# Seam columns of u*B made ahead on ScalarE and POOL and copied in by ScalarE, with 27 products a chunk on POOL, in a one-core Mamba block

## The chip, the cores and the metric

The kernel runs on one core of one Trainium2 chip. The metric is the device time of one execution in microseconds (us); lower is better. The core has a tensor engine (TensorE, PE in the profile), a vector engine (VectorE, DVE), a scalar engine (ScalarE, ACT), GpSimd (POOL) and SyncE (SP), whose queue issues most DMAs. Each engine runs its own list of instructions in order, and they wait for each other on semaphores.

## The reference

Two batches of 2048 rows of width 512 go through a block with adaptive layer norms. The first half is a Mamba mixer, the second a sum of 8 matrices. What matters here is the mixer:

```python
h = layernorm(x) * (1 + ca) + sa
h, gate = split(h @ in_proj_w.T)          # 1024 channels each
h = silu(conv1d_causal(h, 4 taps) + conv_b)
dt, B, C = split(h @ x_proj_w.T)          # 128, 16, 16
dt = softplus(dt @ dt_proj_w.T + dt_proj_b)
for t in rows:                            # per channel e and state n
    s[e, n] = s[e, n] * exp(dt[t, e] * A[e, n]) + (dt[t, e] * h[t, e]) * B[t, n]
    y[t, e] = sum_n s[e, n] * C[t, n]
y = (y + h * D) * silu(gate);  x = x + ga * (y @ out_proj_w.T)
x = x + gb * (sum_r layernorm'(x) @ factors[r] / sqrt(8) + bias)
```

All of it is in 32-bit floats. `u` is dt * h, and `ub` is u * B.

## The kernel before, in words

The 4096 rows are cut into 16 chunks of 256 rows, 8 for each batch. Channels lie on the 128 partitions in 8 tiles, taken as 4 pairs (q = 0 to 3). In a chunk the state recurrence is 64 units, one for each pair q and state n. A unit is one scan over 512 elements: the 256 rows of the pair's first tile and, behind them, the 256 rows of its second. Four units are a quad (g = 0 to 15), two units are a step (s = 0 to 31, so step s lies in quad s // 2).

Each unit takes four operations:

- `decays` (ScalarE, L722): two exponentials fill one of three PSUM banks `decay` with exp(dt * A).
- `make_ub` (POOL, L568): u * B for a whole quad at once, 128x2048, into one of three slots `ub`. It is made two quads ahead.
- `scan` (VectorE, L1426): the recurrence.
- the product with C: on VectorE (`multiply_c`, L1441, into `sc_d`) for the first units of a quad, on POOL (L596, in place in `state_p`) for the last k units of a quad. k is read from the lists `EVEN_POOL`, `ODD_POOL`, `FIRST_POOL` (chunk 0), `FOLD_POOL` (chunk 1) and `LAST_POOL` (chunk 15). TensorE then turns the product back and adds it up in `y_bank` (L1010).

`keep_carry` (ScalarE, L706) keeps the last column of each state for the next chunk. `copy_y` (ScalarE, L811) takes each pair's sums out of `y_bank` at steps 2, 10, 18 and 26 of the pair after it, and TensorE can't begin on the next pair (L1001) before that.

A scan takes only one initial value, so the second tile's carry has to come in otherwise: its first decay is zeroed (L718, or skipped by the exponential), and carry * decay is added to the first column of the second tile in `ub`. That column is the seam. The kernel before does it on POOL: `seam_decays` (ScalarE, L845) writes the decays of the 16 states and a pair into `seam`, `make_seam` (POOL, L554) multiplies them by the carries for two pairs at once, in quads 0 and 4, and behind every `make_ub` POOL adds 128x4 elements of `seam` into `ub` (L582). Chunks 0 and 8 begin a batch and need no seam.

Around the units lies the other work, put between them by hand at given steps: in chunk c the projection and convolution of chunk c + 1 (`project_h` L1085, `copy_h` L766 to L775, `taps` L1481, `add_tap` L1068, `tanh_before` L787, `silu_before` L1490), its dt, B and C (`copy_dt`, `copy_bc`, `soft_dt` L835, with a reload of the activation table), and of chunk c - 1 the gate (`project_gate` L1057, `tanh_gate` L859, `silu_gate` L1500, `turn_sums` L1141, `gate_sums` L1522), the output projection (L1157, `residual_mixer` L1529) and the second half. `copy_h` of the first pair is at step 5, as is `tanh_gate` of the last pair of chunk c - 1; in ScalarE's order of before `copy_h` stands first. B and C of a chunk come back from memory spread over all partitions (`load_b` L340, in two halves), once POOL has used the old ones.

Of the kernel before, what the change touches and what calls it, by code (L numbers as in the profile page):

```python
# [57 lines left out]
EVEN_POOL = (2, 2, 2, 2, 2, 2, 2, 2, 2, 2, 2, 1, 1, 1, 1, 1)  # L58
ODD_POOL = (2, 2, 2, 2, 1, 2, 2, 2, 2, 2, 2, 1, 1, 1, 1, 1)
# [17 lines left out]
NORMS = 2 + LB  # L77

# [38 lines left out]
def seam_count(c):  # L117

    return c - c // PER

# [44 lines left out]
def build(nc, x, win_m, xp_t, dt_t, wo_t, chan, cond_t, wmod, factors, bias, out):  # L165
# [11 lines left out]
    with ExitStack() as ctx:  # L177
# [52 lines left out]
        seam = [sb(f"seam{i}", [P, N, PAIRS]) for i in range(2)]  # L230
        y_rows = sb("y_rows", [P, LB, E])
# [29 lines left out]
        ub_product, seam_decay, seam_made, seam_zeroed = sem("ub_product"), sem("seam_decay"), sem("seam_made"), sem("seam_zeroed")  # L261
# [60 lines left out]
        def _(sp):  # L322
# [10 lines left out]
            def load_b(c, par, h):  # L333

                if c:
                    sp.wait_ge(ub_made, QUADS * c - 2 * (1 - h) - 1)
                sp.wait_ge(bc_stored, 16 * c + 16)
                n0 = h * N // 2
                src = bc_dram[par, 0:1, n0 * ROWS:(n0 + N // 2) * ROWS].to_broadcast([P, N * ROWS // 2])
                sp.dma_start(b_all[:, n0:n0 + N // 2, :].rearrange("p n r -> p (n r)"), src).then_inc(b_loaded[h], 16)  # L340
# [172 lines left out]
        def _(pool):  # L513
# [33 lines left out]
            def make_seam(c, half):  # L547

                qs = slice(2 * half, 2 * half + 2)
                pool.wait_ge(seam_decay, 2 * seam_count(c) - 1 + half)  # L550
                pool.wait_ge(carried, carries_after(UNITS * (c - 1) + N * qs.stop - 1))
                odd = carry[c // PER][:, :, :].rearrange("p n (q j) -> p n q j", j=2)[:, :, qs, 1]
                part = seam[c % 2][:, :, qs]
                pool.tensor_tensor(part, part, odd, ALU.mult).then_inc(seam_made, 1)  # L554

            def make_ub(quad):
# [7 lines left out]
                if q == 0 and n % (N // 2) == 0 or quad == 1:  # L564
# [6 lines left out]
                                   ALU.mult).then_inc(ub_product if c % PER else ub_made, 1)  # L571
                if c % PER == 0:
                    return
                if g == 0:
                    make_seam(c, 0)
                    pool.wait_ge(seam_made, 2 * seam_count(c) - 1)
                if g == 4:
                    make_seam(c, 1)
                    pool.wait_ge(seam_made, 2 * seam_count(c))
                pool.wait_ge(ub_product, QUADS * (seam_count(c) - 1) + g + 1)  # L580
                first = ub[:, slot, :, 1, 0]
                pool.tensor_tensor(first, first, seam[c % 2][:, n:n + QUAD, q], ALU.add).then_inc(ub_made, 1)  # L582
# [67 lines left out]
            def one_round(c, par, la, lc):  # L650
                for g in range(QUADS):
# [7 lines left out]
                    if quad + UB_RING - 1 < QUADS * CHUNKS:  # L659
                        make_ub(quad + UB_RING - 1)  # L660
                    multiply_c(quad)
# [14 lines left out]
                    if la is not None and g == 13:  # L676
                        make_u(c + 1, 0)

# [11 lines left out]
        def _(act):  # L690
# [146 lines left out]

            def seam_decays(c, par, half):
# [3 lines left out]
                wait(act, ub_made, QUADS * (c - 1) - 1)  # L842
# [74 lines left out]
            def one_round(c, par, la, lc):  # L917
                for s in range(STEPS):
                    a = s - H_LATE if c == 0 else s
                    step = STEPS * c + s  # L920
                    pair = 2 * step // N
                    decays(2 * step)
# [18 lines left out]
                    if c == 0 and s in (7, 12):  # L941
                        rows_absolute(s // 12, (0.5, RANK ** -0.5)[s // 12])
                    if s in (4, 6, 12):
                        skip(c, {4: 1, 6: 2, 12: 3}[s])
                    if la is not None:
# [12 lines left out]
                        if s in (27, 31) and (c + 1) % PER:  # L958
                            seam_decays(c + 1, 1 - par, s // 31)
                    if c + 2 < CHUNKS and s == 30:  # L960
                        z_before(c + 2)
                    if lc is not None:
                        if s in (1, 3, 5):
                            tanh_gate(c - 1, {1: 1, 3: 2, 5: 3}[s])
# [443 lines left out]
        def _(dve):  # L1408
            def scan(unit):
# [5 lines left out]
                if unit < QUAD:  # L1415
                    dve.wait_ge(ub_first, unit + 1)
                elif i == 0:
# [312 lines left out]
```

## Time and profile before

| | |
|---|---|
| median of 3 runs | 2021.61 us (2020.21 to 2022.54) |
| the profiled execution, its time | 2025.55 us |
| the profiled execution, its span | 2023.8 us |
| mean granted TensorE clock | 0.973 |
| VectorE busy | 1867.4 us, 92% |
| POOL busy | 1835.7 us, 91% |
| TensorE matmuls busy | 1759.7 us, 87% |
| ScalarE busy | 1517.1 us, 75% |

The span is what the trace covers; the execution's own time is 1.75 us more. Busy time counts the time in which an instruction ran; two short instructions in a row overlap in the records by up to a tenth of a microsecond, so that the distance of their starts is what one costs the engine. Idle time before an instruction is given with what ended it.

### The profile page before, as it was taken

To read this page: it belongs to the slowest core of one execution; us is meant where nothing else is said; L and a number is where in the kernel's file an instruction comes from. 1 tells how busy PE (TensorE), PEld (TensorE's weight loads), DVE (VectorE), ACT (ScalarE), POOL (GpSimd) and SP (SyncE) were. 2 spreads that over 40 slices of the span, in tenths; PEclk is the share of its full clock that TensorE was granted. 3 is DMA by queue.
4 is the path that set the end of the run, shared out by engine and by line. 5 is a ranking of instruction groups with operands and counts; after the bars stand their busy time and mean duration, and the time that the engine had idled before them with its cause. 6 is when DMAs were issued, how large, how long until landed. Compare 5 with 4: busy or idle time off the path is not lost.

```text
span 2023.8 us, 29343 instructions
## 1 busy us (share of the span) xinstructions
PE 1759.7 (87%) x9128; PEld 1312.2 (65%) x9128; DVE 1867.4 (92%) x2240; ACT 1517.1 (75%) x4646; POOL 1835.7 (91%) x925
## 2 busy tenths in 40 slices
PE   7985889889889898988989888898988899898798
PEld 5664757667576765757666675766757576676564
DVE  2799989999999999999999999999999999999995
ACT  3767778697877869777786977878787786878662
POOL 1789999999999999999998999999999999999992
PEclk9897999999999999999999999999999999999798
DMA  4656514132140412304042240403223040311200
GB/s 171 235 114 153 140 48 147 31 121 79 43 143 15 152 47 97 103 30 154 17 141 68 111 141 22 157 22 131 68 73 121 28 156 22 121 53 55 92 27 32
DMA packets 72001, 186.17 MB, mean 92 GB/s; under 512 B 6818, under 2 KB 8482, under 8 KB 63908
## 3 DMA queue, kind: packets, MB, share of 16 engines
q1 hardware_dynamic: 68148, 176.95, 26.3%
q0 software_dynamic: 3696, 7.34, 2.2%
q8 instruction: 73, 1.20, 0.2%
q14 instruction: 84, 0.69, 0.1%
HBM read 172.20 MB, written 12.06 MB: 91 GB/s over the span
## 4 chain that ended last, share of the span: by engine, by line
PE 42%; ACT 19%; POOL 15%; DVE 13%; issue 9%; DMA 1%; DVEq 0%; POOLq 0%; SPq 0%; ACTq 0%
PE y_bank L1010 10%; PE bank_a L1085 10%; PE bank_c L1157 9%; POOL ub L568 8%; ACT decay L722 7%; DVE decay L1426 5%; POOL state_p L596 5%; PE bank_c L1057 4%; DVE state_p L1426 3%; PE bank_a L1068 2%; ACT dt L835 2%; DVE sc_d L1441 2%; ACT L722 2%; ACT hT L737 2%; ACT L835 2%
## 5 line engine op out<-in xcount | busy, mean ns | idle before, releaser
L568 POOL TENSOR_TENSOR ub<-u,b_all 128x2048 f32<-128x2048 f32 x255 | 1160.4, 4551 | 48.5 <-DMA b_all<-bc_scratch 47.4
L722 ACT ACTIVATE decay<-dt,decay_rate 128x256 f32<-128x256 f32 (+1 forms) x2048 | 889.6, 466 | 36.0 <-DVE state_p L1426 34.3
L1426 DVE TENSOR_TENSOR_SCAN decay<-decay,carry,ub 128x512 f32<-128x512 f32 x610 | 763.7, 1277 | 25.8 <-ACT decay L722 23.8
L596 POOL TENSOR_TENSOR state_p<-state_p,c_all 128x1024 f32<-128x1024 f32 (+1 forms) x256 | 498.7, 1948 | 85.3 <-ACT carry L706 82.4
L1426 DVE TENSOR_TENSOR_SCAN state_p<-decay,carry,ub 128x512 f32<-128x512 f32 x414 | 527.4, 1274 | 9.3 <-ACT decay L722 7.2
L1010 PE MATMUL y_bank<-ident,sc_d 128*128 128x128 f32 x2440 | 362.5, 283 | 79.9 <-DVE sc_d L1441 79.5
L1441 DVE TENSOR_TENSOR sc_d<-decay,c_all 128x512 f32<-128x512 f32 x610 | 406.7, 671 | 0.0
L1010 PEld LDWEIGHTS y_bank<-ident,sc_d 128*128 128x128 f32 x2440 | 292.9, 145 | 146.1 <-DVE sc_d L1441 120.8
L706 ACT ACTIVATE carry<-decay 128x2 f32<-128x2 f32 x610 | 100.8, 165 | 264.8 <-DVE sc_d L1441 262.9
L1010 PEld LDWEIGHTS y_bank<-ident,state_p 128*128 128x128 f32 x1656 | 195.7, 143 | 126.9 <-POOL state_p L596 71.7
L1010 PE MATMUL y_bank<-ident,state_p 128*128 128x128 f32 x1656 | 231.0, 279 | 53.2 <-POOL state_p L596 52.0
L1085 PE MATMUL bank_a<-hT,win_h 128*128 128x256 f32 x992 | 240.5, 387 | 32.4 <-DVE hc L1490 30.0
L1057 PE MATMUL bank_c<-hT,win_z 128*128 128x256 f32 x960 | 230.7, 387 | 0.0
L1157 PE MATMUL bank_c<-wo,yg 128*128 128x512 f32 x480 | 223.8, 594 | 0.0
L1085 PEld LDWEIGHTS bank_a<-hT,win_h 128*128 128x128 f32 x992 | 182.3, 193 | 58.7 <-DVE hc L1490 35.7
L1057 PEld LDWEIGHTS bank_c<-hT,win_z 128*128 128x128 f32 x960 | 181.7, 196 | 22.6
L1068 PE MATMUL bank_a<-pre_z,tap_diag 128*128 128x256 f32 x496 | 120.4, 386 | 12.2 <-DVE bank_a L1481 12.2
L1157 PEld LDWEIGHTS bank_c<-wo,yg 128*128 128x128 f32 x480 | 86.6, 191 | 67.0 <-issue 64.8
L1068 PEld LDWEIGHTS bank_a<-pre_z,tap_diag 128*128 128x128 f32 x496 | 92.7, 191 | 39.8 <-DVE bank_a L1481 15.8
L1187 PE MATMUL bank_c<-ffn,hT 128*128 128x512 f32 x240 | 115.9, 605 | 0.0
L1001 PE MATMUL y_bank<-ident,skipped 128*128 128x128 f32 x256 | 42.9, 294 | 71.5 <-ACT y_rows L811 71.5
L718 ACT ACTIVATE decay<-ident 128x1 f32<-128x1 f32 x608 | 103.4, 170 | 0.1
(139 smaller groups left out, 1842.1 us busy)
## 6 DMA issues: line engine op xcount, KB each, us to landing
win_h<-win_m SPq DMA_DIRECT2D x128, 256.0 KB, 2.6
win_z<-win_m SPq DMA_DIRECT2D x128, 256.0 KB, 2.8
b_all<-bc_scratch SPq DMA_DIRECT2D x31, 1024.0 KB, 4.7
c_all<-bc_scratch SPq DMA_DIRECT2D x31, 1024.0 KB, 6.6
xa<-x SPq DMA_DIRECT2D x16, 512.0 KB, 5.0
xc<-x SPq DMA_DIRECT2D x16, 512.0 KB, 3.8
out<-xc SPq DMA_DIRECT2D x15, 512.0 KB, 4.0
ffn<-factors POOLq DMA_DIRECT2D x7, 1024.0 KB, 10.0
```

The source lines that it names most:

```text
L568: pool.tensor_tensor(ub[:, slot, :, :, :], u[:, (PAIRS * c + q) % U_PAIRS, :, :].unsqueeze(1).to_broadcast([P, QUAD, 2, ROWS]), b_all[:, n ...
L596: pool.tensor_tensor(part, part, c_all[:, n + QUAD - k:n + QUAD, :].unsqueeze(2).to_broadcast([P, k, 2, ROWS]), ALU.mult).then_inc(pooled, 1)
L718: act.activation(bk[:, ROWS:ROWS + 1], ident[:, 0:1], ACT.Copy, scale=0.0)
L722: last = act.activation(bk[:, j * ROWS + j:(j + 1) * ROWS], dt[:, pair % DT_PAIRS, j, j:], ACT.Exp, scale=decay_rate[:, e, n:n + 1])
L1010: last = pe.matmul(y_bank[:, at:at + P], tile[:, j, t * P:(t + 1) * P], ident[:, :], start=False, stop=last_of_pair, is_transpose=True, sk ...
L1057: last = pe.matmul(dst[:, j * ROWS:(j + 1) * ROWS], tile[:, k, :], hTc[:, k, :], start=(k == 0), stop=(k == KD - 1))
L1068: last = pe.matmul(h_lane(c, q)[:, j * ROWS:(j + 1) * ROWS], tap_diag[:, i, 2 * q + j, :], pre[q % 2][:, j, k:k + ROWS], start=False, stop ...
L1085: last = pe.matmul(h_lane(c, q)[:, j * ROWS:(j + 1) * ROWS], win_h[i % H_TILES][:, k, :], hT[c % H_RING][:, k, :], start=(k == 0 and j == ...
L1157: last = pe.matmul(bank_c[t][:, :], yg[:, k, t * P:(t + 1) * P], wo[:, k, :], start=(k == 0), stop=(k == KE - 1))
L1187: last = pe.matmul(bank_c[t][:, :], hT[c % H_RING][:, k, t * P:(t + 1) * P], ffn[:, k, :], start=False, stop=(k == KD - 1))
L1426: dve.tensor_tensor_scan(dst, bk[:, :], ub[:, quad % UB_RING, i, :, :].rearrange("p j r -> p (j r)"), carried_in[:, n, 2 * q:2 * q + 1], A ...
L1441: dve.tensor_tensor(sc_d[:, i % D_RING, :, :], bk[:, :].rearrange("p (j r) -> p j r", j=2), c_all[:, n:n + 1, :].to_broadcast([P, 2, ROWS] ...
```

## The change: the seam is added to a column apart, and ScalarE copies it in

POOL no longer adds into `ub`. ScalarE makes the first column of u * B of the second tile apart (`make_column`, into a new buffer `column`, 128x16 for a pair, the first pair in two halves of 128x8). POOL multiplies carries and decays as before (`carry_seam`, now at rounds 13 and 4) and adds the columns to `seam` in four additions a chunk (`add_column`). ScalarE copies 128x4 of `seam` into the slot of `ub` ahead of the first decays of each quad (`add_seam`), and the scan waits for that copy.

With it `make_u` of the next chunk's first pair goes from round 13 to 12 on POOL, `load_b` waits for the columns too, `tanh_gate` at steps 1, 3 and 5 stands ahead of `skip`, `modulate_before`, `tanh_before` and `copy_h` of the same step, and the lists of POOL's products change: quad 7 goes from 2 to 1 and quad 13 from 1 to 2 in both lists, and in the odd chunks quad 4 goes from 1 to 2.

```diff
-EVEN_POOL = (2, 2, 2, 2, 2, 2, 2, 2, 2, 2, 2, 1, 1, 1, 1, 1)
-ODD_POOL = (2, 2, 2, 2, 1, 2, 2, 2, 2, 2, 2, 1, 1, 1, 1, 1)
+EVEN_POOL = (2, 2, 2, 2, 2, 2, 2, 1, 2, 2, 2, 1, 1, 2, 1, 1)
+ODD_POOL = (2, 2, 2, 2, 2, 2, 2, 1, 2, 2, 2, 1, 1, 2, 1, 1)
...
 def load_b(c, par, h):
                 if c:
                     sp.wait_ge(ub_made, QUADS * c - 2 * (1 - h) - 1)
+                    wait(sp, column_made, SEAM_COLUMNS * seam_count(c - 1))
...
+            def add_column(c, qs, columns, ns=slice(0, N)):
+                pool.wait_ge(column_made, SEAM_COLUMNS * (seam_count(c) - 1) + columns)
+                pool.wait_ge(seam_made, 2 * seam_count(c) - 1 + qs.start // 2)
+                part = seam[c % 2][:, ns, qs]
+                pool.tensor_tensor(part, part, column[:, ns, qs], ALU.add).then_inc(seam_added, 1)
...
-                                   ALU.mult).then_inc(ub_product if c % PER else ub_made, 1)
-                if c % PER == 0:
-                    return
-                if g == 0:
-                    make_seam(c, 0)
-                    pool.wait_ge(seam_made, 2 * seam_count(c) - 1)
-                if g == 4:
-                    make_seam(c, 1)
-                    pool.wait_ge(seam_made, 2 * seam_count(c))
-                pool.wait_ge(ub_product, QUADS * (seam_count(c) - 1) + g + 1)
-                first = ub[:, slot, :, 1, 0]
-                pool.tensor_tensor(first, first, seam[c % 2][:, n:n + QUAD, q], ALU.add).then_inc(ub_made, 1)
+                                   ALU.mult).then_inc(ub_made, 1)
...
                         make_ub(quad + UB_RING - 1)
+                    if la is not None and (c + 1) % PER and g == 14:
+                        add_column(c + 1, slice(0, 1), 1, slice(0, N // 2))
+                    if c % PER and g == 0:
+                        add_column(c, slice(0, 1), 2, slice(N // 2, N))
+                    if c % PER and g == 2:
+                        add_column(c, slice(1, 2), 3)
+                    if c % PER and g == 6:
+                        add_column(c, slice(2, 4), 5)
                     multiply_c(quad)
...
-                    if la is not None and g == 13:
+                    if la is not None and g == 12:
                         make_u(c + 1, 0)
+                    if la is not None and (c + 1) % PER and g == 13:
+                        carry_seam(c + 1, 0)
+                    if c % PER and g == 4:
+                        carry_seam(c, 1)
...
+            def add_seam(quad):
+                c, g = quad // QUADS, quad % QUADS
+                q, n = QUAD * g // N, QUAD * g % N
+                act.wait_ge(ub_made, quad)
+                act.wait_ge(seam_added, SEAM_ADDS * (seam_count(c) - 1) + (min(q, 2) + 1 if q or n >= N // 2 else 0) + 1)
+                act.activation(ub[:, quad % UB_RING, :, 1, 0], seam[c % 2][:, n:n + QUAD, q], ACT.Copy).then_inc(ub_seamed, 1)
+
+            def make_column(c, q, ns=slice(0, N)):
+                pair = PAIRS * c + q
+                act.wait_ge(u_made, pair)
+                if q == 0:
+                    act.wait_ge(b_loaded[2 * ns.start // N], 16 * c + 16)
+                wait(act, seam_added, SEAM_ADDS * (seam_count(c) - 1))
+                act.activation(column[:, ns, q], b_all[:, ns, 0], ACT.Identity,
+                               scale=u[:, pair % U_PAIRS, 1, 0:1]).then_inc(column_made, 1)
...
+                    if c % PER and s % 2 == 0:
+                        add_seam(step // 2)
                     decays(2 * step)
...
+                    if c % PER and s == 1:
+                        make_column(c, 0, slice(N // 2, N))
+                    if c % PER and s == 5:
+                        make_column(c, 1)
+                    if c % PER and s == 12:
+                        make_column(c, 2)
+                        make_column(c, 3)
+                    if lc is not None and s in (1, 3, 5):
+                        tanh_gate(c - 1, {1: 1, 3: 2, 5: 3}[s])
                     if s in (4, 6, 12):
                         skip(c, {4: 1, 6: 2, 12: 3}[s])
...
+                        if s == 28 and (c + 1) % PER:
+                            make_column(c + 1, 0, slice(0, N // 2))
...
-                        if s in (1, 3, 5):
-                            tanh_gate(c - 1, {1: 1, 3: 2, 5: 3}[s])
...
+                elif i == 0 and quad // QUADS % PER:
+                    dve.wait_ge(ub_seamed, seamed_count(quad))
                 elif i == 0:
                     dve.wait_ge(ub_made, quad)
```

## Rows read from the trace of the kernel before

**Rows 1.** Part 1 of the page: busy time of each engine.

```profile
PE 1759.7 (87%) x9128; PEld 1312.2 (65%) x9128; DVE 1867.4 (92%) x2240; ACT 1517.1 (75%) x4646; POOL 1835.7 (91%) x925
```

**Rows 2.** VectorE's waits in chunk 4 (571 to 689 us): us, times, longest.

```profile
DVE decay L1426 <- ACT decay L722: 1.0, 3, 0.4
DVE xc L1529 <- PE bank_c L1157: 0.9, 1, 0.9
DVE bank_a L1481 <- ACT bank_a L775: 0.8, 1, 0.8
DVE yg L1500 <- ACT tanh_s L859: 0.4, 1, 0.4
DVE yg L1522 <- PE bank_c L1141: 0.4, 1, 0.4
```

**Rows 3.** VectorE's waits in chunk 5 (689 to 809 us).

```profile
DVE yg L1500 <- ACT tanh_s L859: 1.9, 1, 1.9
```

**Rows 4.** All waits of the execution, and POOL's in chunks 4 and 5.

```profile
DVE yg L1500 <- ACT tanh_s L859: 15.6, 13, 1.9
...
DVE xc L1529 <- PE bank_c L1157: 12.8, 14, 0.9
...
POOL state_p L596 <- ACT carry L706: 8.2, 8, 2.3
```

**Rows 5.** POOL in order of time (start, us, idle before) at quad 8 of chunk 4.

```profile
621.15 4.53 POOL L568 TENSOR_TENSOR ub<-u,b_all 128x2048 f32<-128x2048 f32 x1
625.91 2.37 POOL L596 TENSOR_TENSOR state_p<-state_p,c_all 128x1024 f32<-128x1024 f32 x1
```

**Rows 6.** ScalarE in order of time, steps 1 and 5 of chunk 4, seam decays.

```profile
569.24 0.59 ACT L859 ACTIVATE tanh_s<-bank_c 128x512 f32<-128x512 f32 x1
...
581.53 0.19 ACT L766 ACTIVATE pre_z<-hist 128x6 f32<-128x6 f32 x1
581.62 0.58 ACT L767 ACTIVATE pre_z<-bank_a 128x512 f32<-128x512 f32 x1
...
583.21 0.59 ACT L859 ACTIVATE tanh_s<-bank_c 128x512 f32<-128x512 f32 x1
583.69 0.88 ACT L722 ACTIVATE decay<-dt,decay_rate 128x256 f32<-128x256 f32 x2
...
679.53 0.51 ACT L845 ACTIVATE seam<-decay_rate,dt 128x16 f32<-128x16 f32 x2
```

**Rows 7.** TensorE in order of time, steps 2 to 3 of chunk 4.

```profile
571.25 0.63 PE L1001 MATMUL y_bank<-ident,skipped 128*128 128x128 f32 x4 [2.03 <-ACT y_rows L811]
...
581.25 1.89 PE L1057 MATMUL bank_c<-hT,win_z 128*128 128x256 f32 x8
```

**Rows 8.** VectorE in order of time, steps 5 and 6 of chunk 4.

```profile
584.44 0.87 DVE L1481 SCALAR_TENSOR_TENSOR bank_a<-pre_z,conv,bank_a 128x256 f32<-128x256 f32 x2
585.22 2.46 DVE L1426 TENSOR_TENSOR_SCAN decay<-decay,carry,ub 128x512 f32<-128x512 f32 x2
```

**Rows 9.** ScalarE and VectorE in order of time, steps 27 to 31 of chunk 4.

```profile
666.92 0.67 DVE L1441 TENSOR_TENSOR sc_d<-decay,c_all 128x512 f32<-128x512 f32 x1
...
677.62 0.86 ACT L722 ACTIVATE decay<-dt,decay_rate 128x256 f32<-128x256 f32 x2
678.51 1.29 DVE L1426 TENSOR_TENSOR_SCAN decay<-decay,carry,ub 128x512 f32<-128x512 f32 x1
```

**Rows 10.** Windows at step 2 of chunks 4 and 5: busy, the granted clock.

```profile
571.00:573.00 2.00, 1.75 (x14) 1.75 (x15) 1.92 (x2) 1.97 (x8) 1.05 (x3) 1.00 0.91 298
691.00:693.00 2.00, 2.00 (x9) 1.81 (x8) 2.00 (x3) 0.95 (x4) 2.00 (x1) 0.50 0.86 347
```

**Rows 11.** POOL in order of time, first and last of 11 quads of chunk 1.

```profile
221.78 4.56 POOL L568 TENSOR_TENSOR ub<-u,b_all 128x2048 f32<-128x2048 f32 x1
...
294.06 4.53 POOL L568 TENSOR_TENSOR ub<-u,b_all 128x2048 f32<-128x2048 f32 x1
```

**Rows 12.** Waits of the first half of chunk 15 (1880 to 1945 us).

```profile
PE y_bank L1010 <- POOL state_p L596: 8.6, 4, 4.6
```

More of the change, by code:

```diff
@@ L77 @@
 NORMS = 2 + LB
+SEAM_COLUMNS, SEAM_ADDS = PAIRS + 1, PAIRS
 def wait(eng, sem, value):
@@ L119, in seam_count, with seamed_count @@
     return c - c // PER
+def seamed_count(quad):
+    c, g = quad // QUADS, quad % QUADS
+    return QUADS * (seam_count(c) - 1) + g + 1
 def products_after(unit):
@@ L230, in build @@
         seam = [sb(f"seam{i}", [P, N, PAIRS]) for i in range(2)]
+        column = sb("column", [P, N, PAIRS])
         y_rows = sb("y_rows", [P, LB, E])
@@ L260, in build @@
         skip_turned, y_copied = sem("skip_turned"), sem("y_copied")
-        ub_product, seam_decay, seam_made, seam_zeroed = sem("ub_product"), sem("seam_decay"), sem("seam_made"), sem("seam_zeroed")
+        ub_seamed, seam_decay, seam_made, seam_zeroed = sem("ub_seamed"), sem("seam_decay"), sem("seam_made"), sem("seam_zeroed")
+        seam_added, column_made = sem("seam_added"), sem("column_made")
         a_full = [sem(f"a_full{i}") for i in range(2)]
@@ L545, in make_u, with carry_seam @@
                 pool.tensor_tensor(u[:, pair % U_PAIRS, :, :], dt[:, pair % DT_PAIRS, :, :], hc[:, k, :], ALU.mult).then_inc(u_made, 1)
-            def make_seam(c, half):
+            def carry_seam(c, half):
                 qs = slice(2 * half, 2 * half + 2)
@@ L836, in soft_dt @@
                 last.then_inc(dt_made, 1)
+            def add_seam(quad):
+                c, g = quad // QUADS, quad % QUADS
+                q, n = QUAD * g // N, QUAD * g % N
[10 more added lines that the diff above has]
+                               scale=u[:, pair % U_PAIRS, 1, 0:1]).then_inc(column_made, 1)
             def seam_decays(c, par, half):
                 act.wait_ge(dt_made, PAIRS * c + 2 * half + 2)
-                wait(act, ub_made, QUADS * (c - 1) - 1)
+                wait(act, ub_seamed, QUADS * seam_count(c - 2))
                 for q in (2 * half, 2 * half + 1):
```

## The prediction

> **What bounds the kernel now.** I read the page's busy times first, then VectorE's waits chunk by chunk, then each engine's list in order of time around those waits. The page shows VectorE and POOL about equally loaded, TensorE close behind [rows 1]; that alone doesn't say which of them a gain on POOL would help. VectorE's waits do. In chunk 4, some 118 us long, it idles 3.5 us, for decays of ScalarE, for the output projection, for the convolution's copy, for the gate's tanh and for the turned sums [rows 2]. None of these waits is for `ub` or for a seam. So VectorE sets the pace in most of the chunk, with short stretches where TensorE and ScalarE set it. POOL is the one that waits: 8.2 us in chunks 4 and 5 together, for the carries kept by ScalarE [rows 4], 4.1 us a chunk.
>
> Chunk 5 differs from chunk 4 in one thing: the wait for the gate's last tanh is 1.9 us and not 0.4 [rows 3]. The windows at step 2 say why. In chunk 4 TensorE has its full clock (1.00, the 2.4 GHz level), in chunk 5 it has 0.50 (1.2 GHz) for the same work, behind a gap in which it waited for `y_rows` [rows 10]; that gap is 2.03 us in chunk 4 as well [rows 7], where it brought no fall. Over the execution this wait is 15.6 us in 13 times [rows 4], which is 7 chunks of 1.9 and 6 of 0.4. A fall of the clock there costs 1.5 us.
>
> **POOL's side.** An addition of 128x4 and its wait cost POOL 0.23 us: `ub` ends at 621.15 + 4.53 = 625.68, the product starts at 625.91 [rows 5]. 16 a chunk are 3.7 us in 14 seam chunks. Four additions of up to 128x32 come back; I take 0.25 each, 1.0 a chunk (at least the same 0.23; at most 0.4, if a wait shows). POOL gains 2.7 us a chunk. In chunks 2 to 14 that is worth 0 on the path, since POOL's waits already exceed it; the extra work goes into longer waits. It could be worth up to 0.3 a chunk where TensorE waits for POOL's product. In chunk 1 POOL works without a pause over 11 quads, 221.78 to 294.06 [rows 11], and TensorE waits for it; there it gives 11 x 0.23 less three additions, about 1.8 us. In the first half of chunk 15 TensorE waits 8.6 us for POOL [rows 12]; some 9 quads of it give 9 x 0.23 less two or three additions, 1.5 us. Together -3.3 us, between 0 and -7.4 (if all 32 quads of both chunks count, and the columns cost nothing).
>
> **The moved products.** A product on VectorE is 0.67 us in the record [rows 9], about 0.6 between starts. Quad 4 in the odd chunks and quad 7 lie ahead of `residual_mixer`, where VectorE waits 0.9 us for TensorE's output projection, in chunk 4 [rows 2] and 14 times in all, 12.8 us and never more than 0.9 [rows 4]: in even chunks (two products of quad 4 on POOL) and odd ones (one) alike. So one product more or less there is hidden by that wait: 0, and +0.6 if the wait were gone. Quad 13's product leaves VectorE at step 27, behind which it runs without a stop to step 31. But there ScalarE is just in time: the decays that start at 677.62 end at 678.48, and the scan starts at 678.51 [rows 9], after soft_dt's table loads and `z_before`, with no pause of ScalarE in between. ScalarE saves one carry and one zeroing there and gets two `add_seam` and one half column. So the 0.6 mostly turns into a wait for that decay: I take -0.1 a chunk, between 0 and -0.6.
>
> **ScalarE's new operations.** Two seam decays of 128x16 with a pointer as scale take 0.51 us together [rows 6], 0.2 for each further one; a column is the same form. A small copy costs 0.09 (581.53 to 581.62). 16 copies and five columns are 16 x 0.09 + 5 x 0.2 = 2.4 us a chunk. ScalarE is 75% busy [rows 1], so it has room on the whole, and their semaphores are early: POOL makes `ub` two quads ahead. What counts is where they stand. At steps 1 and 2, `make_column`, `tanh_gate` and one `add_seam` now lie ahead of the copy of `y_bank`, which TensorE waits for (2.03 us) [rows 7]. Column and copy are 0.3, and `tanh_gate`, which started at 569.24 behind `modulate_before` [rows 6], may wait a little for the gate's sums: I take +0.4 a chunk for TensorE's start and all that follows it, between 0.1 and 0.6. Elsewhere (step 22 and the decays of rows 2) a copy of 0.09 ahead of a late decay costs up to 0.1; POOL's earlier product gives about that back: 0.
>
> **The new order at step 5.** This is the largest term. `copy_h` runs from 581.53 to the tanh's start at 583.21, 1.68 us [rows 6]. The tanh needs the gate's last matmuls, and these run 581.25 + 1.89 = 583.14 [rows 7]. So the tanh can't start before 583.15: with the new order it gains 0.06, and `copy_h`, whose input was ready 1.6 us earlier, now runs behind it, about 583.7 to 585.4. VectorE's `taps` (584.44) and the decays of unit 12 (583.69, needed by the scan at 585.22) [rows 6, 8] come behind `copy_h`. The decays end at about 585.4 + 0.9 = 586.25, the scan is 1.0 us later. Of that the wait for the turned sums (0.4) [rows 2] is absorbed. Behind it, queued on ScalarE, are `skip`, the decays of units 13 to 15 and the second `copy_h`; ScalarE catches up in its own waits. `silu_before` of step 8, for which TensorE waits, passes the rest on. Net +0.6 a chunk, between 0 (if there is slack that I don't see) and +1.2.
>
> **The sum.** For a chunk of 2 to 14: +0.4 + 1.0 - 0.4 - 0.1 = +0.9 us, times 13 = +11.7. With -3.3 from chunks 1 and 15: +8.4 us. The profiled execution took 2025.55 us, 1.75 over its span and 3.9 over the median of the runs; the sum is a difference and I put it on the median: 2021.6 + 8.4 = 2030.0 us. A change of under 0.2% (4 us) is about what a measurement can't tell from none.
>
> **The rivals.**
> *The moved product pays (faster).* Its place is step 27: if ScalarE's chain there comes out shorter, because a carry and a zeroing are gone, all of the 0.6 counts; 13 x 0.6 = 7.8 us. If besides this the order at step 5 costs nothing, the result is 2021.6 - 7.8 - 3.3 = 2010.5. It decides from the point where `copy_h` behind the tanh costs under 0.5 us a chunk. For it: POOL had no room at quad 13 and now gets it. Against it: the 0.03 us between decay and scan.
> *The clock falls in other chunks.* The gap ahead of step 2 grows from 2.03 to some 2.4 us. If it brings the fall in all 13 chunks, 6 more cost 6 x 1.5 = 9 us: 2039. If the new spacing avoids all of them, 7 x 1.5 = 10.5 us come back: 2019.5, no change to be seen. Seven of 13 with the same gap show that its length doesn't decide alone. The Trainium skill ("TensorE: Matmul & The Clock Gate", the section on HAM oscillation) says that pauses of TensorE bring it back to half its clock, again and again where they recur; by that rule the longer gap speaks for 2039, and the trace agrees only in part.
> *Waiting for the seam.* ScalarE now waits for POOL in order: if `ub` or an `add_column` is late, decays stop. `ub` is ahead by several us at most quads, least in quads 12 and 17. A wait of 0.5 us in five quads a chunk would give 2030 + 14 x 2.5 = 2065.
> *Nothing moves.* The new copies, POOL's relief and the order offset each other: 2022.
>
> **How the numbers follow.** The forecast, 2025.7 to 2036: 0.38. More falls of the clock, or late seams: 0.12, slower. The moved product pays: 0.28, faster. The clock's falls avoided, or all offset: 0.22, of which 0.17 within 0.2% and 0.03 and 0.02 to its sides. So faster 0.31, same 0.17, slower 0.52. The range reaches from the faster rival to the clock's worst, 2008 to 2040; the forecast's own is 2025.7 to 2036.
>
> **What the profile after would show.** If I am right: L1481 or the scan behind it waits about 1 us for ScalarE at step 5 in each chunk 2 to 14, and the wait for the tanh (L1500) is not shorter; L1522's wait is gone; TensorE's wait at L1001 is 2.3 to 2.6; POOL's waits for the carries grow from 4.1 to some 6 us a chunk; the scan at step 31 waits some 0.4 us for its decay. Wrong if the tanh's wait falls to 0 (then the gate's matmuls end earlier than the profile models), if the scan of step 31 has no wait, or if the count of chunks with the clock at 0.5 is far from 7.

## The result, and the profile after

| | before | after |
|---|---|---|
| median of 16 runs each, same chips | 2021.79 us | 2025.66 us |
| lowest to highest | 2020.21 to 2024.84 | 2023.23 to 2034.52 |
| the profiled execution | 2025.55 us, span 2023.8 | 2029.70 us, span 2027.9 |
| mean granted TensorE clock | 0.973 | 0.975 |

The ratio is 1.0026, with the interval [1.0016, 1.0036] (the two medians alone give 1.0019): the kernel became slower, by 3 to 7 us, just beyond what its measurement can tell. The forecast was 2030.0.

One execution of the kernel hc_first_q7, below, the profiled one, ran with a mean clock of 0.84 and took 2133.69 us; its ratio leaves it out.

Part 1 of the page of after, against [rows 1]:

```profile
PE 1756.6 (87%) x9128; PEld 1309.0 (65%) x9128; DVE 1868.9 (92%) x2234; ACT 1548.3 (76%) x4928; POOL 1807.0 (89%) x757
```

POOL lost 29 us of work, ScalarE took up 31 us, VectorE has the same. (One product of 1.2 us in each odd chunk came back to POOL, so the loss isn't 14 times 2.7.) In the steady chunks POOL's relief bought next to nothing, and its own waits show where it went. Chunks 4 and 5 (571 to 809 us), in us, times, longest:

```profile
POOL state_p L602 <- ACT carry L724: 14.8, 10, 3.8
```

It was 8.2 us [rows 4]. By the prediction's sum the relief is 2.7 us a chunk, and the wait for the carries grew by 3.3 a chunk.

For the path I take the start of the second `residual_mixer` (step 17) as a mark in each chunk. From mark to mark is a period. The periods of one kernel come in a few sharp values, so a difference of 0.1 us can be read. Two marks of after, VectorE in order of time (start, us, what ran, idle before):

```profile
630.65 0.69 DVE L1578 TENSOR_TENSOR xc<-bank_c,xc 128x512 f32<-128x512 f32 x1 [0.69 <-PE bank_c L1204]
...
749.95 0.69 DVE L1578 TENSOR_TENSOR xc<-bank_c,xc 128x512 f32<-128x512 f32 x1 [0.69 <-PE bank_c L1204]
```

749.95 - 630.65 = 119.30. Before has 118.41 in its quiet chunks and 120.07 where TensorE's clock falls; after has 119.29, 120.97 with one fall, 122.48 with two. Chunk 2 is the period from chunk 1's mark to its own. The two profiled spans add up so:

| us | before | after | difference |
|---|---|---|---|
| start, to the mark in chunk 1 | 269.93 | 267.02 | -2.9 |
| chunks 2 to 14, 13 periods | 1556.93 | 1568.24 | +11.3 |
| of it 13 quiet periods | 1539.3 | 1550.8 | +11.4 |
| of it falls, and the irregular chunks 2, 8 and 9 | 17.6 | 17.5 | -0.1 |
| chunk 15 | 112.52 | 111.36 | -1.2 |
| end | 84.42 | 81.28 | -3.1 |

So the change costs 0.88 us in every steady chunk, and the ends are some 7 us shorter; how much of the 7 is the change's is asked further down. Where the 0.88 arises is seen at steps 1 to 5. ScalarE in order of time in chunk 5, against [rows 6]:

```profile
685.61 0.30 ACT L871 ACTIVATE column<-b_all,u 128x8 f32<-128x8 f32 x1
685.82 0.57 ACT L895 ACTIVATE tanh_s<-bank_c 128x512 f32<-128x512 f32 x1
686.29 1.00 ACT L755 ACTIVATE hT<-bank_a,mods 128x256 f32<-128x256 f32 x2
687.19 0.20 ACT L862 ACTIVATE ub<-seam 128x4 f32<-128x4 f32 x1
687.29 0.87 ACT L740 ACTIVATE decay<-dt,decay_rate 128x256 f32<-128x256 f32 x2
688.08 0.58 ACT L829 ACTIVATE y_rows<-y_bank 128x512 f32<-128x512 f32 x1
...
700.74 0.60 ACT L895 ACTIVATE tanh_s<-bank_c 128x512 f32<-128x512 f32 x1 [1.33 <-PE bank_c L1104]
701.23 0.20 ACT L784 ACTIVATE pre_z<-hist 128x6 f32<-128x6 f32 x1
...
702.01 0.99 ACT L793 ACTIVATE bank_a<-bank_a,conv 128x256 f32<-128x256 f32 x2
702.93 0.21 ACT L862 ACTIVATE ub<-seam 128x4 f32<-128x4 f32 x1
703.02 0.87 ACT L740 ACTIVATE decay<-dt,decay_rate 128x256 f32<-128x256 f32 x2
```

At step 5 `tanh_gate` now stands ahead of `copy_h`, and ScalarE waits 1.33 us at it for the gate's matmuls, with `copy_h` (0.09 + the copies, 1.7 us) queued behind although its input is there. The small operations are cheap in place: from `add_seam` at 687.19 to the decay at 687.29 is 0.10, from the column at 685.61 to the tanh 0.21. TensorE in order of time, chunk 5, against [rows 7]:

```profile
688.81 0.63 PE L1048 MATMUL y_bank<-ident,skipped 128*128 128x128 f32 x4 [2.33 <-ACT y_rows L829]
...
698.81 1.89 PE L1104 MATMUL bank_c<-hT,win_z 128*128 128x256 f32 x8
...
712.56 1.99 PE L1115 MATMUL bank_a<-pre_z,tap_diag 128*128 128x256 f32 x8 [1.43 <-DVE bank_a L1530]
...
716.70 1.99 PE L1132 MATMUL bank_a<-hT,win_h 128*128 128x256 f32 x8 [2.15 <-DVE hc L1539]
```

The gate's matmuls end at 698.81 + 1.89 = 700.70, and the tanh starts 0.04 later: it can't be earlier in either order. In before it started 0.07 behind them. VectorE, chunk 5, against [rows 8]:

```profile
701.37 0.69 DVE L1549 SCALAR_TENSOR_TENSOR yg<-tanh_s,bank_c 128x512 f32<-128x512 f32 x1 [0.36 <-ACT tanh_s L895]
...
703.04 0.88 DVE L1530 SCALAR_TENSOR_TENSOR bank_a<-pre_z,conv,bank_a 128x256 f32<-128x256 f32 x2 [0.99 <-ACT bank_a L793]
703.93 2.47 DVE L1475 TENSOR_TENSOR_SCAN decay<-decay,carry,ub 128x512 f32<-128x512 f32 x2
...
706.89 1.27 DVE L1571 TENSOR_TENSOR yg<-bank_c,yg 128x512 f32<-128x512 f32 x2
```

The wait of 0.99 at `taps` is new; the one for the turned sums (`gate_sums`) is gone. The clock, in windows of after (length; busy of PE, PEld, DVE, ACT, POOL; granted clock; DMA share; GB/s), the first two at step 2 of chunks 5 and 7, the last at step 8 of chunk 7:

```profile
689.00:691.00 2.00, 2.00 (x16) 1.91 (x15) 1.81 (x3) 1.53 (x5) 1.06 (x1) 1.00 1.02 385
927.00:929.00 2.00, 1.60 (x8) 1.63 (x9) 1.81 (x2) 2.00 (x8) 0.48 (x1) 0.52 0.89 288
958.00:960.00 2.00, 2.00 (x7) 1.52 (x7) 2.00 (x3) 0.84 (x2) 2.00 (x1) 0.50 0.00 0
```

In chunks 7, 10 and 11 the clock falls twice, 1.00 to 0.50 (2.4 to 1.2 GHz): at step 2 and at step 8, behind `project_h`'s wait of 2.15 us. In chunks 2 to 14 after has six falls at step 2 and four at step 8. Before has seven at step 2 and one at step 8, in chunk 3, where step 2 has none:

```profile
478.46 3.60 PE L1085 MATMUL bank_a<-hT,win_h 128*128 128x256 f32 x8 [2.14 <-DVE hc L1490]
```

The price of the second fall, TensorE and VectorE in order of time in chunk 7:

```profile
956.80 2.82 PE L1132 MATMUL bank_a<-hT,win_h 128*128 128x256 f32 x8 [2.15 <-DVE hc L1539]
962.97 1.29 DVE L1475 TENSOR_TENSOR_SCAN decay<-decay,carry,ub 128x512 f32<-128x512 f32 x1 [2.07 <-ACT decay L740]
```

2.82 us for the same eight matmuls that took 1.99 in chunk 5, and a scan behind it that waits 2.07 for its decay: 122.48 - 120.97 = 1.5 us for the second fall, 1.7 for the first.

### The profile page after: what moved, and what is told of

It reads as the page before. It is cut to its first block and busy times, and to the rows that moved or that the text cites. A ratio compares the mean times of both kernels' runs of the same rounds, so it can differ in the third digit from the quotient of the medians.

```text
span 2027.9 us, 29762 instructions
## 1 busy us (share of the span) xinstructions
PE 1756.6 (87%) x9128; PEld 1309.0 (65%) x9128; DVE 1868.9 (92%) x2234; ACT 1548.3 (76%) x4928; POOL 1807.0 (89%) x757
## 5 line engine op out<-in xcount | busy, mean ns | idle before, releaser
L1475 DVE TENSOR_TENSOR_SCAN decay<-decay,carry,ub 128x512 f32<-128x512 f32 x604 | 756.9, 1279 | 31.6 <-ACT decay L740 29.6
L602 POOL TENSOR_TENSOR state_p<-state_p,c_all 128x1024 f32<-128x1024 f32 (+1 forms) x256 | 513.6, 2006 | 138.6 <-ACT carry L724 135.7
L1475 DVE TENSOR_TENSOR_SCAN state_p<-decay,carry,ub 128x512 f32<-128x512 f32 x420 | 535.9, 1276 | 6.2 <-ACT decay L740 4.3
L1057 PEld LDWEIGHTS y_bank<-ident,sc_d 128*128 128x128 f32 x2416 | 286.0, 144 | 155.4 <-DVE sc_d L1490 130.1
L1057 PEld LDWEIGHTS y_bank<-ident,state_p 128*128 128x128 f32 x1680 | 200.5, 144 | 104.5 <-issue 52.1
L1057 PE MATMUL y_bank<-ident,state_p 128*128 128x128 f32 x1680 | 235.7, 280 | 32.1 <-POOL state_p L602 32.1
```

Source lines behind the costliest of these rows:

```text
L602: pool.tensor_tensor(part, part, c_all[:, n + QUAD - k:n + QUAD, :].unsqueeze(2).to_broadcast([P, k, 2, ROWS]), ALU.mult).then_inc(pooled, 1)
L1057: last = pe.matmul(y_bank[:, at:at + P], tile[:, j, t * P:(t + 1) * P], ident[:, :], start=False, stop=last_of_pair, is_transpose=True, sk ...
L1475: dve.tensor_tensor_scan(dst, bk[:, :], ub[:, quad % UB_RING, i, :, :].rearrange("p j r -> p (j r)"), carried_in[:, n, 2 * q:2 * q + 1], A ...
```

## The experiments

Twelve kernels were run, in three groups of four, each group beside runs of the kernel before on the same chip. Ratios are to these. The kernel after wasn't run again beside them, and the median of before moved by up to 2 us between groups, so kernels of two groups are compared by their ratios. "Quiet period" is the period of a chunk without a fall, from the profiled execution.

| kernel | ratio, interval | median us | before beside it | quiet period |
|---|---|---|---|---|
| before | 1 | 2021.79 | | 118.41 |
| after | 1.0026 [1.0016, 1.0036] | 2025.66 | 2021.79 | 119.29 |
| order_back | 0.9968 [0.9956, 0.9979] | 2016.22 | 2023.40 | 118.64 |
| order_only | 1.0027 [1.0016, 1.0037] | 2028.66 | 2023.40 | 118.95 |
| lists_back | 1.0020 [1.0006, 1.0033] | 2025.69 | 2023.40 | 119.62 |
| no_adds | 0.9972 [0.9961, 0.9983] | 2017.80 | 2023.40 | 118.24 |
| order_back_col | 0.9966 [0.9954, 0.9978] | 2016.47 | 2023.77 | 118.46 |
| gap_short | 0.9942 [0.9924, 0.9959] | 2013.58 | 2023.77 | 117.93 |
| gap_before | 0.9977 [0.9967, 0.9987] | 2018.05 | 2023.77 | 117.98 |
| lists_only | 0.9983 [0.9974, 0.9991] | 2020.00 | 2023.77 | 117.88 |
| copies_twice | 1.0062 [1.0048, 1.0076] | 2036.49 | 2023.31 | 119.99 |
| quad7_back | 1.0043 [1.0031, 1.0056] | 2032.15 | 2023.31 | 118.95 |
| hc_first | 0.9832 [0.9818, 0.9845] | 1988.96 | 2023.31 | 117.34 |
| hc_first_q7 | 0.9808 [0.9794, 0.9821] | 1983.90 | 2023.31 | |

### The parts of the change

The first group takes the change apart: the order of `tanh_gate`, the lists, the additions.

**order_back** is after, with `tanh_gate` where before has it. **order_only** is before with that one move alone.

```diff
-                    if lc is not None and s in (1, 3, 5):
-                        tanh_gate(c - 1, {1: 1, 3: 2, 5: 3}[s])
                     if s in (4, 6, 12):
...
                     if lc is not None:
+                        if s in (1, 3, 5):
+                            tanh_gate(c - 1, {1: 1, 3: 2, 5: 3}[s])
```

> The changed kernel with one thing undone: tanh_gate at steps 1, 3 and 5 stands again behind skip, modulate_before and copy_h. Theory (the order costs 0.6 to 0.9 us in each of 14 chunks): copy_h of step 5 runs again while the gate's matmuls do, taps don't wait, and the chunk period without a fall of the clock goes from 119.29 to some 118.6 us; the time is 8 to 11 us below the changed kernel, some 2016 us, 5 below the kernel before. Rival (the cost is the load of 21 more operations on ScalarE in each chunk, wherever they stand): the period stays at 119.2 and the time at 2025. Second rival (falls of TensorE's clock make the whole difference): the period without a fall is 118.4 in all kernels, and the time follows their count alone.

> The kernel before with nothing but tanh_gate of steps 1, 3 and 5 moved ahead of skip, modulate_before and copy_h. Theory: period without a fall of the clock from 118.41 to 119.0 us (1.0 at the taps less 0.4 at the turned sums), 8 us over the kernel before, some 2030. Rival (load on ScalarE): no change, 118.4 and 2022.

Measured: order_back takes 2016.22 us, 7.2 less than the before beside it. Its ratio is 0.58% below that of after, some 12 us. The quiet period is 0.65 shorter, which is 8.5 us in 13 chunks; in the profiled executions another 5.2 us are falls that it has less, so the falls are a part of the gain, though not the whole of it, as the second rival had it. The wait of 0.99 at `taps` of step 5 is gone. order_only is 0.27% slower than before, quiet period 118.95, +0.54. The order alone makes the change a loss.

**lists_back** is after with the lists of before.

```diff
-EVEN_POOL = (2, 2, 2, 2, 2, 2, 2, 1, 2, 2, 2, 1, 1, 2, 1, 1)
-ODD_POOL = (2, 2, 2, 2, 2, 2, 2, 1, 2, 2, 2, 1, 1, 2, 1, 1)
+EVEN_POOL = (2, 2, 2, 2, 2, 2, 2, 2, 2, 2, 2, 1, 1, 1, 1, 1)
+ODD_POOL = (2, 2, 2, 2, 1, 2, 2, 2, 2, 2, 2, 1, 1, 1, 1, 1)
```

> The changed kernel with the two lists of POOL's products of before. Theory (quad 13's product was worth 0.1 a chunk because the decays of step 31 come late, quads 4 and 7 nothing): the same within 2 us, at most 1.3 us slower, 2025 to 2027. Rival (the product moved at quad 13 pays its whole 0.6 in 13 chunks, and the loss elsewhere is larger): 8 us slower, 2033.

The time is that of after, as expected, but for another reason: the quiet period is 119.62, 0.33 longer, so the lists are worth 0.33 a chunk. The profiled execution had fewer falls (6.9 us in 13 chunks against 17.5), which would hide it; that the other executions have fewer as well isn't shown.

**no_adds** is before without the 224 additions into `ub` (and `make_seam` ahead of the product), so the second tile's carry never enters.

```diff
+                if c % PER and g in (0, 4):
+                    make_seam(c, g // 4)
...
-                                   ALU.mult).then_inc(ub_product if c % PER else ub_made, 1)
-                if c % PER == 0:
-                    return
...
-                pool.tensor_tensor(first, first, seam[c % 2][:, n:n + QUAD, q], ALU.add).then_inc(ub_made, 1)
+                                   ALU.mult).then_inc(ub_made, 1)
```

> The kernel before without the 224 additions of the seam into ub on POOL, and nothing in their place (the states lose the carry into the second tile of each pair); the 28 multiplications by the carries stay, ahead of the ub they stood behind. It prices POOL's relief by itself. Theory: nothing in chunks 2 to 14, whose period stays at 118.4; 3 us in chunks 1 and 15 and up to 3 in the tail: 2016 to 2019. Rival (POOL is a bound in every chunk): 14 x 3.7 us less, toward 1975.

0.28% faster, 5.6 us, as expected, for 3.7 us of POOL's time taken away in each of 14 chunks. Of the profiled span's 9.3 us, the quiet periods are 13 x 0.17 = 2.2, the rest lies in the falls (14.9 us against 17.6), the start and chunk 15 (-1.7 and -1.0) and the end. For a kernel with the lists of before that is about the ceiling of what POOL's relief can be worth.

### The clock's falls

The second group aims at the gap ahead of step 2 and at the question whether POOL needed its relief.

**order_back_col** is order_back with the half column of step 1 one step later. **gap_short** is order_back_col with a `modulate_before` of step 1 at step 2 as well. **gap_before** is before with that second move alone.

```diff
-                    if c % PER and s == 1:
+                    if c % PER and s == 2:
                         make_column(c, 0, slice(N // 2, N))
```

```diff
-                        if a == M_AT[c > 0]:
+                        if (s == 2 if c else a == M_AT[0]):
                             modulate_before(c + 1, 1)
```

> The changed kernel with tanh_gate in its old order and make_column of step 1 moved to step 2, behind the copy of y_bank. Theory (the column ahead of that copy delays TensorE by its 0.2 us): TensorE's wait at step 2 from 2.33 to 2.1 us, the period without a fall of the clock 0.2 to 0.3 below the 118.64 of the kernel with the order alone, 2012 to 2014 us. Rival (the column is hidden, and the 0.23 a chunk that stay over the kernel before come from the copies ahead of the decays): 118.6 and 2016.

> As the kernel with the old order and the column at step 2, and modulate_before of the second bank (two operations, 1.0 us) goes from step 1 to step 2, behind the copy of y_bank, in chunks from 1 on. TensorE's wait ahead of L1048 shrinks to about 1.1 us. Theory (the clock falls at step 2 because of this wait, 1.6 us a time, and the wait for the tanh of 0.4 is its tail): no fall of the clock at step 2 in any chunk, periods all alike near 118.0, 2016 less 7 x 1.6 less 13 x 0.4 = some 2000 us. Rival (the fall comes from what lies around the gap and stays, or the hT that comes 1 us later holds up the projection): falls in half of the chunks as before, 2012 or more.

> The kernel before with only modulate_before of the second bank moved from step 1 to step 2, behind the copy of y_bank, in chunks from 1 on. Theory: wait of TensorE from 2.03 to 1.0, no fall of the clock at step 2 in chunks 2 to 14, 2022 less 7 x 1.6 less 13 x 0.4 = some 2006 us. Rival: falls as before, 2018 to 2022.

The column moved away shortens the quiet period by 0.18, a little less than expected; the time doesn't move (2012 to 2014 was expected, and 2016.47 is order_back's within the interval). gap_short and gap_before have quiet periods of 117.93 and 117.98 and, in chunks 3 to 14, no fall at step 2. But the time falls by 2.9 us against order_back_col and by 5.7 against before, where 16 or so were expected: 11 and 9 of their chunks now have a fall at step 8, most with a period of 119.62 to 119.68. TensorE in order of time at step 8 of gap_short, chunk 3:

```profile
468.58 2.00 PE L1115 MATMUL bank_a<-pre_z,tap_diag 128*128 128x256 f32 x8 [0.77 <-DVE bank_a L1530]
...
472.72 3.16 PE L1132 MATMUL bank_a<-hT,win_h 128*128 128x256 f32 x8 [2.15 <-DVE hc L1539]
```

and the window there:

```profile
473.00:475.00 2.00, 2.00 (x7) 1.59 (x7) 2.00 (x3) 0.87 (x2) 2.00 (x2) 0.60 0.00 0
```

Without the fall at step 2, the clock falls at step 8, behind a wait of 2.15 that was there all along and had a fall once in before. My expectation failed in taking the falls as belonging to one gap.

**lists_only** is before with the new lists (the diff of lists_back, reversed).

> The kernel before with the new lists of POOL's products and nothing else. Theory (the moved product of quad 13 is worth 0.33 a chunk by the kernel with the lists alone undone, and POOL has enough room at quad 13 without its relief): the period without a fall goes from 118.41 to 118.1, 4 us less, 2018. Rival (POOL needs the relief to take the product): ub of the next chunk's first quads comes late, 2024 or more.

0.17% faster, quiet period 117.88, 0.53 shorter than before, where 118.1 was expected: POOL, with all its additions, carries quad 13's second product. So the moved product doesn't need the seam work's relief, and the lists are worth 0.53 a chunk without the seam work and 0.33 with it. Here 11 of the chunks from 3 on have a fall (eight at step 2, three at step 8, periods of 119.49 to 119.57). The 13 quiet periods give 6.9 us, and the falls take 6.2 of them back.

### The sizes, and both gaps

**copies_twice** is after with every copy of `add_seam` made a second time, into a buffer that nobody reads. **quad7_back** is after with quad 7 at 2 in both lists.

```diff
+                act.activation(extra[:, g, :], seam[c % 2][:, n:n + QUAD, q], ACT.Copy)
                 act.activation(ub[:, quad % UB_RING, :, 1, 0], seam[c % 2][:, n:n + QUAD, q], ACT.Copy).then_inc(ub_seamed, 1)
```

> The changed kernel with each of the 224 copies add_seam preceded by a second one of the same 128x4 into a buffer that nobody reads. It prices the copies. Theory (of the 0.66 us a chunk that the seam work costs on ScalarE, 0.18 is the column ahead of the copy of y_bank and the rest the 16 copies ahead of late decays): the period without a fall of the clock goes from 119.29 up by 0.4 to 0.5, 6 us more, 2032. Rival (the copies hide in ScalarE's idle time, and the rest of the 0.66 is something else, a wait or POOL's order): 119.3 to 119.4 and 2026.

> The changed kernel with quad 7 back at 2 products on POOL (28 a chunk and not 27). Theory (the product that went to VectorE at quad 7 isn't hidden: the stretch from silu_before of step 8 to the second residual_mixer of step 17 is 33.99 us with it and 33.54 without): that stretch 33.54 again, the period 119.29 - 0.45 = 118.85, 6 us less than the changed kernel, 2020. Rival (POOL is then too late for the quads behind it, 9 to 14): the stretch shrinks but the rest grows by as much, 2025.

Sixteen more copies a chunk cost 0.70 in the quiet period, more than the 0.4 to 0.5 expected, and with more falls 0.36% against after by the ratios, 7 us. quad7_back has the shorter quiet period, 118.95 (-0.34), but takes no less time: its ratio is 0.17% above that of after, with intervals that overlap, where 6 us less were expected. Its trace has four chunks of 122.1, with two falls; its 13 periods add up to 1566.1 us, only 2.1 less than after and not 4.4, and the stretch up to the first mark is 2.9 us longer (269.94), of which 0.9 lies ahead of the first scan. So the period was predicted nearly right and the time wrongly. The falls took half of the gain; the rest stays open.

**hc_first** is gap_short with one more move, on VectorE: the last `gate_sums` of step 8 stands behind `silu_before`, for which `project_h` waits. **hc_first_q7** is that with quad 7 at 2.

```diff
-                        if 6 <= s <= 8:
+                        if 6 <= s <= 7 or la is None and s == 8:
                             gate_sums(c - 1, s - 5)
...
                             silu_before(c + 1, SILU_AT[c > 0][a])
+                        if c and s == 8:
+                            gate_sums(c - 1, 3)
```

> As the kernel with modulate_before at step 2, and on VectorE the last gate_sums of step 8 behind silu_before of that step, for which TensorE waits 2.1 us. Theory (where TensorE sets the pace from step 8 to 17, an earlier start of it counts in full): TensorE's wait there 1.5 us, the period without a fall from 117.9 to 117.3, and fewer falls at step 8; 2013.6 less 8 to 20 us, 1994 to 2006. Rival (the stretch begins with VectorE's own work, which only trades places): no change, 2013.

> As the one before, and quad 7 at 2 products on POOL. Theory: another 0.45 a chunk, 13 x 0.45 = 6 us under it, if the falls of the clock stay as many. Rival (POOL late): the same or slower.

hc_first takes 1988.96 us, 1.7% less than before and below the 1994 to 2006 that were expected. TensorE in order of time, chunk 7, with both gaps:

```profile
913.12 0.63 PE L1048 MATMUL y_bank<-ident,skipped 128*128 128x128 f32 x4 [1.22 <-ACT y_rows L829]
...
936.60 2.00 PE L1115 MATMUL bank_a<-pre_z,tap_diag 128*128 128x256 f32 x8 [0.77 <-DVE bank_a L1530]
...
940.15 1.99 PE L1132 MATMUL bank_a<-hT,win_h 128*128 128x256 f32 x8 [1.55 <-DVE hc L1539]
```

The marks of chunks 4 and 5, VectorE in order of time:

```profile
621.36 0.69 DVE L1578 TENSOR_TENSOR xc<-bank_c,xc 128x512 f32<-128x512 f32 x1 [0.68 <-PE bank_c L1204]
...
738.70 0.69 DVE L1578 TENSOR_TENSOR xc<-bank_c,xc 128x512 f32<-128x512 f32 x1 [0.68 <-PE bank_c L1204]
```

and windows at steps 2 and 8 of chunk 4:

```profile
568.00:570.00 2.00, 2.00 (x17) 1.85 (x16) 2.00 (x2) 1.62 (x5) 2.00 (x1) 1.00 0.58 160
600.00:602.00 2.00, 2.00 (x16) 1.69 (x15) 2.00 (x4) 1.49 (x7) 2.00 (x2) 1.00 0.37 116
```

The gaps are 1.22 and 1.55 us instead of 2.33 and 2.15, the clock stays at 1.00, and from chunk 3 on every period is 117.34 or just under. Of the 24.6 us against gap_short, 13 x 0.59 = 7.7 are the quiet period, and gap_short's 11 falls at 1.7 are 18. hc_first_q7 is 5 us better still, 1983.90, nearly the 6 expected, which fits that a quiet period's gain arrives in the time where there are no falls. No trace of it is read here. That both gaps had to shrink is not shown in full: no kernel with the second gap alone made shorter was run.

## Why the prediction was right, point by point

**The sum.** +0.9 a chunk was forecast for chunks 2 to 14, and +0.88 was measured. That it fits so well is partly luck: the new order came out as forecast, but two other terms, the seam work outside steps 1 and 2 and the lists, were off by about 0.3 and 0.2, and offset each other.

To see where a chunk gains and loses, I take the start of VectorE's first scan of a step, in us behind the mark, in a quiet period (the chunk at whose mark it ends stands in brackets):

| first scan of | before (12) | order_only (14) | lists_back (13) | after (14) |
|---|---|---|---|---|
| step 26 of the chunk before | 29.59 | 29.57 | 29.45 | 29.38 |
| step 28 of the chunk before | 36.81 | 36.79 | 36.76 | 36.08 |
| step 0 | 51.38 | 51.35 | 51.62 | 50.87 |
| step 3 | 61.03 | 60.99 | 61.56 | 60.80 |
| step 5 | 67.52 | 67.49 | 68.06 | 67.30 |
| step 7 | 76.99 | 77.53 | 78.20 | 77.44 |
| the next mark | 118.41 | 118.95 | 119.62 | 119.29 |

**The new order at step 5** (net +0.6, +1.0 less the absorbed 0.4): confirmed, with +0.54 in order_only and +0.65 in order_back. In the table it arises between steps 5 and 7 alone (67.49 to 77.53 against 67.52 to 76.99), so the moves at steps 1 and 3 cost nothing. The wait of 0.99 at `taps` and the missing one for the turned sums are the two halves.

**The seam work on ScalarE** (+0.4 for steps 1 and 2, 0 elsewhere): the first part right, the second mis-sized. lists_back less order_only, both with the new order and the old lists, is 119.62 - 118.95 = +0.67; order_back less lists_only, both with the old order and the new lists, is 118.64 - 117.88 = +0.76. By the table, lists_back is 0.12 ahead of order_only at step 26, 0.27 behind at step 0, 0.57 at step 3 and 0.67 at step 7. (The 0.12 is POOL's relief, below.) So steps 1 and 2 cost 0.30, within the 0.1 to 0.6 of the forecast, and 0.18 of it is the half column ahead of the copy of `y_bank` (order_back_col), about the 0.2 that I gave it. Steps 26 to 31 cost another 0.39, in the stretch where [rows 9] shows ScalarE just in time, and step 5, with its column, 0.10. "Elsewhere 0" is the step that failed: outside steps 1 and 2 it cost 0.49, less the 0.12. That it is the copies ahead of late decays is inferred. copies_twice has a like price, 0.70 for sixteen more copies, all of it ahead of step 8. Sixteen at 0.10 would be 1.6, so half or more of their time was hidden. The copies and the columns weren't taken apart outside step 1.

**The lists** (-0.1, quads 4 and 7 at 0): mis-sized, and half wrong in reason. From the mark to `silu_before` at step 8, lists_back takes 86.07 and after 85.31: quad 13's product gives 0.76, more than its 0.6 (and 0.96 in lists_only against before), and 0.61 of it arises between steps 26 and 28, where the moved product stood. The wait at step 31's scan that I expected to eat it (0.4) is 0.17:

```profile
677.37 1.29 DVE L1475 TENSOR_TENSOR_SCAN decay<-decay,carry,ub 128x512 f32<-128x512 f32 x1 [0.17 <-ACT decay L740]
```

From step 8 to the next `residual_mixer`, in quiet chunks, it is 33.54 in before, no_adds, order_only and lists_back alike and 33.98 in after, order_back and lists_only: the product of quad 7 on VectorE costs 0.44, though `residual_mixer`'s wait of 0.9 [rows 2, 4] seemed to hide it. That wait only shrank to 0.69. The step that failed is taking this wait as slack: what it waits for came 0.44 later as well. That TensorE's work there hangs on VectorE's in the same stretch is inferred from this. Quad 4's product did cost nothing: lists_back has two of its products on POOL in even chunks and one in odd ones, and chunks 10 to 13 take 119.61 or 119.62 alike. Net -0.33.

**POOL's relief** (0 in chunks 2 to 14, -3.3 in 1 and 15): right for the steady chunks, 0.17 at most even with all additions gone; in no_adds it is there from step 23 on (17.80 against 17.98), and lists_back is 0.11 ahead of order_only at the same place. At the ends it was mis-sized. From the first scan of chunk 1 to that of chunk 2, the four kernels with the additions on POOL (before, order_only, gap_before, lists_only) take 127.1 to 127.3 us, and the nine without them whose traces are read 122.2 to 123.4: 4.6 less in no_adds and 4.9 in after, where 1.8 was forecast. That is more than the 3.7 of a chunk's additions, so something else moved with them, which wasn't looked for. In chunk 15 the first half gave 0.6 of the 1.5. The rest of the ends isn't the seam's as far as the runs tell. Ahead of the first scan after is 1.0 us earlier (59.48 against 60.52), and quad7_back, the same kernel up to there, has 60.42. From chunk 15's mark to the last scan before takes 53.13 us, and every other kernel read here 51.0, order_only and lists_only too. Behind the last scan the kernels lie between 30.0 and 31.6 whichever way their seam is made, after 1.0 below before.

**The median.** +8.4 was forecast, and 3.9 came by the medians and 5.3 by the ratio. The 2025.66 us lies at the lower edge of the forecast's own range, 2025.7 to 2036. In the profiled executions, 4.1 us apart, the steady chunks have the forecast's cost, and the ends are 7 us shorter and not 3.3. As some 4 us of this aren't the seam's, it stays open whether the other executions came to the same difference in the same way.

**The rivals.** *The moved product pays*: true as a part (0.76 at its place), but its condition, that `copy_h` behind the tanh costs under 0.5, failed by a little (0.54 to 0.65). *The clock falls in other chunks*: it did, in a way I hadn't foreseen. In the profiled executions the falls cost the same (17.6 and 17.5 us, with what is irregular in chunks 2, 8 and 9). But after runs up to 2034.5 us, with a mean clock of 0.970 in that run and 0.976 in the one of 2023.23: its spread goes with the clock. A fall at step 2 costs 1.7 us, not the 1.5 that I read from one wait. Which chunks have one isn't settled by anything that was run. The same gap of 2.33 us has one in chunk 7 and none in chunk 5. The rule of the Trainium skill cited in the prediction ("TensorE: Matmul & The Clock Gate", HAM oscillation), that pauses bring the half clock back again and again, fits hc_first, where both recurring gaps are shorter and no fall is left in the steady chunks; it doesn't tell why a gap has a fall in one chunk and not in the next. *Waiting for the seam*: ScalarE's copy waits for POOL twice, both in chunk 1 (2.2 us for a column's addition, 1.6 for `ub`), and never in chunks 2 to 15.

**What the profile after would show**: the wait at `taps` or the scan of about 1 us, the unshortened wait for the tanh, the wait for the turned sums gone, TensorE's gap of 2.33 (2.3 to 2.6) and about 7 chunks with a fall (7 of chunks 2 to 14, 3 of them with two) came out. POOL's waits for the carries went to 7.4 a chunk, not 6; 4.1 and the relief of 2.7 would have been 6.8 by the prediction's own numbers. The scan of step 31, 0.17 where 0.4 was forecast, was the miss.

## What to carry to other kernels

An instruction that waits on an in-order engine should stand behind work that is ready: `tanh_gate` couldn't start earlier, so moving it ahead of `copy_h` brought it 0.03 us closer to the gate's matmuls (0.04 behind them and not 0.07) and cost 0.54 a chunk. Moving work off the busiest-looking engine is worth next to nothing where that engine already waits for others (3.7 us of POOL a chunk were worth 0.17 in the steady chunks), and much more where it works without a pause (4.6 us in chunk 1). Compare periods of single chunks, which show 0.1 us, ahead of medians, which the clock's falls blur by several us. And a wait ahead of a step is slack only if what it waits for doesn't move with the work that you put there.

## What the runs showed of the hardware that was not expected

TensorE's clock fell from 1.00 to 0.50 behind recurring waits of 2.0 to 2.3 us, in some chunks and not in others with the same wait, at 1.5 to 1.7 us each in most chunks (1.3 in the last of gap_short). When the first gap was shortened to 1.1 or 1.2 us (gap_before, gap_short), the falls moved to the second, whose wait of 2.15 us hadn't changed, and came there in 9 and 11 chunks instead of one. With the two at 1.22 and 1.55 us (hc_first) they stayed away, and 13 chunks took 1528.75 us against 1556.93 before. A change that makes a quiet chunk shorter can so gain next to nothing: in lists_only the quiet periods gave 6.9 us and the falls took 6.2. The small operations cost ScalarE's queue 0.10 us (128x4 copy) and 0.21 (128x8 with a pointer as scale), though their records are 0.20 and 0.30 long.
